# First cross-attention of a two-layer kernel: scores and values on parts of the TensorE array, spreading on GpSimd, half of the normalising on ScalarE, another order of the steps

## The reference

```python
def _layernorm(x, axis=-1, eps=1e-05):
    m = jnp.mean(x, axis=axis, keepdims=True)
    v = jnp.var(x, axis=axis, keepdims=True)
    return (x - m) / jnp.sqrt(v + eps)

def _L0_xattn_ref(x, y, Wq, bq, Wkv, bkv, Wo, bo):    # x: 2x1024x256, y: 2x77x192, 16 heads of 16
    q = (jnp.einsum('bld,ed->ble', x, Wq) + bq).reshape(b, l, h, dh)
    kv = (jnp.einsum('bmc,ec->bme', y, Wkv) + bkv).reshape(b, m, h, 2 * dh)
    k, v = (kv[..., :dh], kv[..., dh:])
    att = jax.nn.softmax(jnp.einsum('blhd,bmhd->blmh', q, k) * scale, axis=2)
    out = jnp.einsum('blmh,bmhd->blhd', att, v).reshape(b, l, d)
    return jnp.einsum('bld,ed->ble', out, Wo) + bo
# x = x + attention(layernorm(x)), then x = x + experts(layernorm(x)), and the second layer
```

## Time and profile before

| | before |
|---|---|
| runs, median (lowest to highest) | 885.86 us (884.95 to 891.11), 3 runs |
| profiled execution, its own time | 889.84 us |
| its span | 887.7 us |
| busy in the span | PE 724.3 us, DVE 584.6, POOL 355.8, ACT 294.8 |

### The profile page before, as it was taken

The page is one execution under the profiler, slowest core; times in us unless marked ns, Lnnn a source line. Parts: engine busy times, 40 slices in busy tenths (PEclk is TensorE's granted clock), DMA queues, the critical chain, the costliest instruction groups (busy, mean ns, idle before and its releaser), DMA issues.

```text
span 887.7 us, 10616 instructions
## 1 busy us (share of the span) xinstructions
PE 724.3 (82%) x3332; PEld 417.2 (47%) x3332; DVE 584.6 (66%) x1732; ACT 294.8 (33%) x641; POOL 355.8 (40%) x372
## 2 busy tenths in 40 slices
PE   4689877864798998989979866868798899999972
PEld 3456544562344444444547623323253374647651
DVE  3888887435756373462657788999795497664265
ACT  2354333210372451815412253555420212021210
POOL 2344434103588685685410246787700021112020
PEclk9999999955898997988979977998889799999996
DMA  8910000210122221121288100020010000000002
GB/s 219 400 31 1 1 12 3 80 62 24 53 72 72 69 81 49 65 81 58 78 256 317 44 2 0 1 95 1 0 48 0 1 1 0 1 0 1 0 1 95
DMA packets 33086, 52.77 MB, mean 59 GB/s; under 512 B 8718, under 2 KB 21582, under 8 KB 32776
## 3 DMA queue, kind: packets, MB, share of 16 engines
q1 hardware_dynamic: 28040, 36.76, 12.6%
q0 software_dynamic: 4992, 15.34, 5.1%
HBM read 36.62 MB, written 15.47 MB: 59 GB/s over the span
## 4 chain that ended last, share of the span: by engine, by line
PE 54%; DVE 25%; POOL 6%; issue 6%; ACT 5%; DMA 2%; POOLq 1%; SPq 0%; DVEq 0%; ACTq 0%
PE ps L459 50%; DVE arena L1883 4%; DVE arena L1880 3%; ACT arena L934 2%; DVE arena L1496 2%; DVE arena L1492 2%; DVE arena L329 2%; DMA arena<-scr_z,idsU 2%; DVE kp L1385 1%; DVE arena L1385 1%; DVE arena L1391 1%; POOL arena L1274 1%; POOL scr_g L1266 1%; PE ps L514 1%; DVE X L1391 1%
## 5 line engine op out<-in xcount | busy, mean ns | idle before, releaser
L459 PE MATMUL ps<-arena 64*32 64x32 f32 (+6 forms) x2296 | 543.6, 396 | 29.9 <-DVE arena L1609 8.7
L459 PEld LDWEIGHTS ps<-arena 128*128 128x128 f32 (+3 forms) x2296 | 267.3, 164 | 231.5 <-issue 182.7
L934 ACT ACTIVATE arena<-ps 128x256 f32<-128x256 f32 (+6 forms) x255 | 120.5, 487 | 280.5 <-PE ps L459 136.0
L324 POOL TENSOR_SCALAR rstd<-mv 128x4 f32<-128x4 f32 (+2 forms) x34 | 14.6, 430 | 236.8 <-DVE mv L318 183.4
L1736 DVE TENSOR_TENSOR arena<-ps,arena 128x512 f32<-128x512 f32 x39 | 27.0, 691 | 103.3 <-ACT arena L1048 91.1
L1232 POOL TENSOR_TENSOR arena<-arena 128x616 f32<-128x616 f32 x32 | 40.2, 1256 | 80.0 <-DVE arena L1504 80.0
L1266 POOL DMA_INDIRECT scr_g<-arena,destU x39 | 50.1, 1285 | 37.7 <-DVE arena L1736 30.4
L1259 POOL DMA_INDIRECT arena<-scr_z,idsU x39 | 45.9, 1177 | 40.8 <-PE ps L652 28.7
L1883 DVE MATCH_REPLACE8 arena<-arena 128x77 f32<-128x77 f32 x256 | 54.1, 222 | 0.0
L1048 ACT ACTIVATE arena<-ps 128x512 f32<-128x512 f32 x39 | 23.3, 597 | 92.2 <-PE ps L459 92.0
L988 ACT ACTIVATE arena<-arena 128x616 f32<-128x616 f32 x32 | 23.0, 717 | 75.7 <-DVE arena L1496 75.7
(11 more groups left out here) (196 smaller groups left out, 988.9 us busy)
## 6 DMA issues: line engine op xcount, KB each, us to landing
arena<-in_w1t SPq DMA_DIRECT2D x8, 1024.0 KB, 14.0
arena<-scr_g SPq DMA_DIRECT2D x8, 1024.0 KB, 7.9
X<-in_x SPq DMA_DIRECT2D x2, 1024.0 KB, 5.9
scr_z<-arena SPq DMA_DIRECT2D x4, 512.0 KB, 3.3
...
```

The lines of the kernel that those rows point to most:

```text
L459: return pe.matmul(o, l, r, start=first, stop=final)
L934: return a.activation(o, i, ACT.Copy)
```

## The change

Scores: each of the two matmuls of a unit takes only the 64 rows of `qT` and `kblk` that aren't zero for its four heads, so one lies on partitions 0 to 63 and the other on 64 to 127. Values: instead of five matmuls with 128 output columns, eight with 32 output columns (two heads) each, over the two chunks that hold those heads' keys; their outputs lie on the four groups of 32 PSUM partitions. All values of a group are now in one place of the order. The first spreads of the keys (batch 0) stay on DVE; the other six go to GpSimd, ahead of its loop, with a semaphore of their own (`vblk_ready`). `kvT` shares the memory of `OT`. `norm_A` of blocks 2 and 3 and `norm_B` of blocks 0 and 1 move to ScalarE as activations with scale rstd and bias -mean x rstd (`nmr`), which GpSimd prepares in `ln_shift`. ScalarE has `put_P` ahead of the exponential; DVE has sum and reciprocal of u - 1 (`total`) ahead of the maximum of u. `queries(0, 1)` and several of the other parts stand at other steps, and `project`'s second pair goes to bank 6 of its own. In the diff below `turn_P`'s buffer index (PBUF, still 4) is left out, and so are removed lines that the functions above show.

```diff
@@ -48,6 +48,8 @@
...
+LAG = 3
+PBUF, LATE = LAG + 1, LAG - 2
...
@@ -144,10 +146,10 @@
...
-        Pb = ra.take(4, GW)
-        kvT = Region(ra.at).take(2, 2, NB * S2)
+        Pb = ra.take(PBUF, GW)
...
-        mxA, smA = ra.take(4, HG), ra.take(4, HG)
+        mxA, smA, nmr = ra.take(PBUF, HG), ra.take(PBUF, HG), ra.take(2 * TB)
+        kvT = OT.rearrange("p g n -> p (g n)")[:, 0:4 * NB * S2].rearrange("p (a b n) -> p a b n", a=2, b=2)
...
@@ -496,10 +498,11 @@
                     pe.wait_ge(s["scores_read"], u - 1)
                 if t == 0:
                     pe.wait_ge(s["qT_sb"], 2 * j + g + 1)
-                    pe.wait_ge(s["kblk_ready"], 2 if j < 2 else 8)
+                    pe.wait_ge(*((s["kblk_ready"], 2) if j < 2 else (s["vblk_ready"], 6)))
                 for c in range(2):
-                    ins = mm(ps[:, 2 * (u % 2) + c, 0:BW], qT[:, j % 2, g, t * P:(t + 1) * P],
-                             kblk[:, g, j // 2, c * BW:(c + 1) * BW], True, True)
+                    half = slice(c * P // 2, (c + 1) * P // 2)
+                    ins = mm(ps[:, 2 * (u % 2) + c, 0:BW], qT[half, j % 2, g, t * P:(t + 1) * P],
+                             kblk[half, g, j // 2, c * BW:(c + 1) * BW], True, True)
                 ins.then_inc(s["scores_ready"], 1)
             def turn_P(u):
@@ -525,26 +528,21 @@
                     ins = pe.transpose(ps[0:m, 6, c * P:(c + 1) * P], vblk[:, g, b, ch * P:ch * P + m], ident[:])
                 ins.then_inc(s["vk_ps"], 1)
...
+            def values(j, g):
+
+                pe.wait_ge(s["pt_sb"], turned_all(8 * j + 4 * g + 3))
+                for r in range(2):
+                    for q in range(4):
+                        m, cols = vkeys(q + r), slice(32 * q, 32 * q + 32)
+                        ins = mm(ps[cols, 6, :], vk[0:m, j // 2, g, q + r, cols], PT[0:m, g, q + r, :], r == 0, r == 1)
+                ins.then_inc(s["oT_ps"], 1)
             def project(j, pair):
                 pe.wait_ge(s["oT_sb"], 2 * j + 2)
...
                 for t in (2 * pair, 2 * pair + 1):
                     for g in range(2):
...
+                        ins = mm(ps[:, 6 + pair, (t % 2) * D:(t % 2) * D + D], OT[:, g, t * P:(t + 1) * P], wo0[:, g, :],
                                  g == 0, g == 1)
                 ins.then_inc(s["oA_ps"], 1)
@@ -553,55 +551,61 @@
             turn_z(0, 0, 7)
             turn_z(0, 1, 6)
             queries(0, 0, 7)
...
+            for S in range(NU + LAG):
                 j, st = S // 8, S % 8
                 ahead = j + 1 < NBLK
                 if S < NU:
                     scores_A(S)
...
+                if S >= LAG:
+                    turn_P(S - LAG)
                 if 1 <= S <= 5:
                     turn_v(S - 1)
...
+                if S >= NU:
+                    pass
+                elif st == 0:
                     if j >= 2:
...
+                        pe.wait_ge(s["xA_done"], 2 * j - 2)
+                    else:
+                        pe.wait_ge(s["qT_sb"], 1 + 2 * j)
+                    queries(j, 1, 7)
+                elif st == 1 and ahead:
+                    pe.wait_ge(s["qT_sb"], 2 * j + 2)
+                    turn_z(j + 1, 0, 7)
+                    if j:
+                        pe.wait_ge(s["oT_sb"], 2 * j - 1)
+                        turn_z(j + 1, 1, 6)
                 elif st == 2:
...
+                    if j == 0:
+                        pe.wait_ge(s["zTA_sb"], 3)
+                        turn_z(1, 1, 7)
+                    elif ahead:
+                        queries(j + 1, 0, 7)
+                elif S == 3:
+                    queries(1, 0, 7)
+                j, st = (S - LATE) // 8, (S - LATE) % 8
+                ahead = j + 1 < NBLK
+                if j < 0 or S >= NU + LATE:
+                    continue
+                if st == 2 and j:
                     if ahead:
...
+                        pe.wait_ge(s["zTA_sb"], 2 * j + 4)
+                    else:
+                        pe.wait_ge(s["oT_sb"], 2 * j - 1)
+                    values(j - 1, 1)
+                elif st == 4 and j:
+                    project(j - 1, 0)
+                elif st == 5 and j:
                     if ahead:
...
+                        pe.wait_ge(s["qT_sb"], 2 * j + 3)
+                    project(j - 1, 1)
                 elif st == 6:
                     if j:
...
+                        pe.wait_ge(s["xA_done"], 2 * j - 1)
+                    else:
+                        pe.wait_ge(s["vk_sb"], 5)
+                    values(j, 0)
+            pe.wait_ge(s["oT_sb"], 2 * NBLK - 1)
+            values(NBLK - 1, 1)
             project(NBLK - 1, 0)
             project(NBLK - 1, 1)
             stage_end("tensor", pe)
@@ -976,34 +980,57 @@
                     a.wait_ge(s["oA_ps"], 2 * j)
                 copy(OT[:, g, :], bank(6)).then_inc(s["oT_sb"], 1)
+            def scaled(dst, n, k):
+                return a.activation(dst, X[:, n, :], ACT.Identity, bias=nmr[:, k:k + 1], scale=rstd[:, k:k + 1])
+
+            def norm_A2(j, tiles):
+                a.wait_ge(s["lnA_rstd"], j + 1)
+                a.wait_ge(s["zTA_ps"], 2 * j)
+                for t in tiles:
+                    scaled(zA[:, t, :], 4 * j + t, 4 * (j % 2) + t).then_inc(s["zA_ready"], 1)
+
+            def norm_B2(j, tiles):
+                a.wait_ge(s["lnB_rstd"], j + 1)
+                for t in tiles:
+                    scaled(zB[:, 4 * j + t, :], 4 * j + t, TB + 4 * j + t).then_inc(s["zB_ready"], 1)
+
             for i in range(2):
                 put_z(0, i, 7 - i)
...
+            put_q(0, 0, 7)
+            for S in range(NU + LAG):
                 j, st = S // 8, S % 8
                 ahead = j + 1 < NBLK
+                if S >= LAG:
+                    put_P(S - LAG)
+                if 1 <= S <= 5:
+                    put_v(S - 1)
                 if S < NU:
                     a.wait_ge(s["scores_read"], S + 1)
...
+                    a.activation(Pb[:, S % PBUF, :], Pb[:, S % PBUF, :], ACT.Exp, scale=1.0 / math.sqrt(DH0))\
                         .then_inc(s["probs_exp"], 1)
...
+                    if st == 0:
+                        put_q(j, 1, 7)
+                    if st == 1 and ahead:
+                        put_z(j + 1, 0, 7)
+                        if j:
+                            put_z(j + 1, 1, 6)
+                    if st == 2 and ahead:
+                        if j:
+                            put_q(j + 1, 0, 7)
+                        else:
+                            put_z(1, 1, 7)
                     if S == 3:
...
+                        put_q(1, 0, 7)
+                    if (S - LATE) % 8 == 2 and j:
                         put_o(j - 1, 1)
...
+                    if (S - LATE) % 8 == 6:
+                        put_o(j, 0)
+                    if S in (6, 7):
+                        norm_A2(2, (2 * (S - 6), 2 * (S - 6) + 1))
+                    elif S in (11, 12):
+                        norm_A2(3, (2 * (S - 11), 2 * (S - 11) + 1))
+                    elif j >= 2 and st in (3, 4) and "B" in stages:
+                        norm_B2(j - 2, (2 * (st - 3), 2 * (st - 3) + 1))
             put_o(NBLK - 1, 1)
             stage_end("scalar", a)
             if "B" in stages:
@@ -1212,11 +1239,27 @@
             own.done(p.memset(halfpi[:], math.pi / 2))
             own.settle()
+            def ln_shift(at, stats, count, signal):
+                r, m = rstd[:, at:at + 4], nmr[:, at:at + 4]
+                p.wait_ge(s[stats], count)
+                own.done(p.tensor_scalar(r, mv[:, at:at + 4, 1], EPS, None, ALU.add))
+                own.done(p.tensor_scalar(m, mv[:, at:at + 4, 0], -1.0, None, ALU.mult))
+                own.settle()
+                own.done(p.tensor_tensor(r, r, neghalf[:, 0:4], ALU.pow))
+                own.settle()
+                p.tensor_tensor(m, m, r, ALU.mult).then_inc(s[signal], 1)
+
             def rstd_A(j):
-                ln_rstd(p, own, 4, 4 * (j % 2), "lnA_stats", j + 1, "lnA_rstd")
+                if j < 2:
+                    ln_rstd(p, own, 4, 4 * (j % 2), "lnA_stats", j + 1, "lnA_rstd")
+                else:
+                    ln_shift(4 * (j % 2), "lnA_stats", j + 1, "lnA_rstd")
             def rstd_B(j):
-                ln_rstd(p, own, 4, TB + 4 * j, "lnB_stats", j + 1, "lnB_rstd")
+                if j >= 2:
+                    ln_rstd(p, own, 4, TB + 4 * j, "lnB_stats", j + 1, "lnB_rstd")
+                else:
+                    ln_shift(TB + 4 * j, "lnB_stats", j + 1, "lnB_rstd")
             def bias_A(T):
@@ -1225,20 +1268,32 @@
             rstd_A(0)
             rstd_A(1)
+            p.wait_ge(s["consts_in"], 16 * 9)
+            p.wait_ge(s["kv_sb"], 4)
+            for i, b in ((1, 0), (1, 1), (0, 1)):
+                for g in range(2):
+                    p.tensor_tensor((kblk, vblk)[i][:, g, b, :].rearrange("p (h k) -> p h k", h=HG),
```

(64 more changed lines are left out.)

119 lines of the change are left out of this document (3 added, 116 removed).

## The result

| | before | changed |
|---|---|---|
| runs, median (lowest to highest) | 885.40 us (882.58 to 891.11), 4 runs | 862.48 us (861.03 to 864.02), 4 runs |
| profiled execution, its own time | 889.84 us | 861.57 us |
| its span | 887.7 us | 859.6 us |
| first maximum of the loop | 25.91 | 23.29 |
| end of the last subtraction | 150.98 | 132.45 |

The ratio is 0.973, with a 95% interval of 0.968 to 0.979: faster by 22.9 us, where 18.6 were forecast. The last three rows of the table split what happened in stage A of the two profiled executions: run-up 25.91 - 23.29 = 2.6 us less, loop 125.1 to 109.2, 15.9 less, tail 20.2 to 17.7, 2.5 less; together 21.1 us. Behind stage A the profiled executions differ by another 7.0 us (716.5 and 709.5). Before's profiled execution lies 4.0 us above the median of its first runs, so a part of the 7.0 may be that; what makes them up was not isolated.

What follows compares the result with a forecast made beforehand. It took PE to bound the loop, with DVE close behind and the new bound after the change. 23.1 us saved less 4.5 for the clock gave 18.6 us saved, 867.3 us, with a range of 858 to 880.

Steps and rivals of the forecast that it cites:

- the sum: Whole kernel: 23.1 us saved in the stage, less 4.5 for the clock, so 18.6 us saved and 867.3 us.
- the likeliest case: Whole kernel: the forecast as summed, 864 to 872 us, chance 0.6.
- DVE's cycle: Loop: sum, reciprocal, maximum, subtraction and exponential repeat every 3.35 us, with a 0.79 us hole on DVE.
- PE's work after the change: Loop: with tiles fully overlapping, scores 0.51 us and values 1.72, a block takes 19.9 us, 2.5 a step.
- the mechanism that the prediction made of it: PE: tiles in program order barely overlap, scores 0.77 us, values 3.9, 3.3 a step; within a rival of chance 0.18.
- such a cost at a change of the tiling mode: PE: two or three drains of 0.27 us a step would lift 2.5 us to at most 3.3.
- Extras: DVE in the loop: `split_bias` 6.0 us and statistics 1.3 beyond the holes, 7.3 in all.
- The clock in the loop: Loop: PE's granted clock may fall in steps 25, 26 and 28, costing 0 to 6 us, 1.5 taken.
- Run-up: Before the loop: scores wait only for the first query copy, so the first maximum comes at 23.1 us instead of 25.91.
- ScalarE's queue: Loop: copies and normalisations (0.4 us each) ahead of or behind the exponential delay nothing, at most 1 us.
- Tail: From the last subtraction to the next stage's first transposes: 12.2 us against 20.2, before any clock cost.
- the clock's cost: Tail: values and projections at half the clock, bounds 0 and 5.5 us, 3 taken.

Runs made afterwards that it cites:

- e12: The changed kernel again, with only a blank line ahead of it: 858.85 us, ratio 0.971 to the kernel before.
- e11: The kernel before with six spreads moved to GpSimd, norms to ScalarE, and tiled scores and values, in the old orders: 867.39 us, ratio 0.977.
- e4: The changed kernel with four idle 512-column matmuls added on PE in the tail: 854.58 us, ratio 0.966 to the kernel before.
- e6: The changed kernel with the sixteen normalisations moved from ScalarE back to DVE: 864.92 us, ratio 0.973 to the kernel before.
- e7: The changed kernel with the six spreads moved from GpSimd back to DVE: 863.31 us, ratio 0.973 to the kernel before.
- e3: The kernel before with only the tiled scores and values added: 886.01 us, ratio 0.999 to the kernel before.
- e9: The kernel before with only six spreads moved to GpSimd and the norms to ScalarE, no tiles, old orders: 876.22 us, ratio 0.988.
- e8: The changed kernel with ScalarE's exponential back ahead of the copies (`put_P`): 873.04 us, ratio 0.985 to the kernel before.
- e2: The changed kernel with DVE's sum and reciprocal of u-1 back behind the subtraction of u: 851.42 us, ratio 0.962 to the kernel before.

## Why the prediction was right, step by step

The time lies in the range of 858 to 880, 4.8 us below the 867.3 of the sum and 1.5 below the likeliest case of 864 to 872. How it comes about was forecast in the main: a loop set by DVE's cycle of sum, maximum, subtraction and exponential. But the number didn't test the tiles: without them (e1) it would have been 867.0, in the likeliest case itself. By its steps:

- **PE's work after the change.** Four tiles side by side: forecast 1.72 us for the values and 1.9 with the end, measured 1.93; two row tiles: 0.51 of work and 0.82 with the end, measured 0.79. That the tiles overlap is shown. The Trainium skill, "TensorE: Matmul & The Clock Gate", Part 3, has matmuls start and end strictly in program order; the mechanism that the prediction made of it, 3.9 and 0.77 plus the end, is not what these tiles do. But PE's work was put too low, at 1.06 us for scores and transposes of a step, where 0.72 + 0.69 = 1.41 pass from start to start. That is 0.35 a step and 2.8 a block, so 22.7 us a block where 19.9 were forecast. It shows in the busy time: 85% of the loop, part of it at the lower clock, where 70 to 80 were forecast, and 29.64 of 35.00 us at a granted clock of 0.98. The prediction allowed for such a cost at a change of the tiling mode as an upper bound and left it out of the sum. How much of the 0.35 comes from that change no run isolates. In the changed kernel it showed no cost: DVE waited for PE 0.6 us in all.
- **DVE's cycle.** Forecast 3.35 with a hole of 0.79, measured 3.31 with 0.78, and waits for PE down to 0.6 us: right. The 15.6 us of waits that the prediction read from the earlier trace rows were only 8.9 in the loop; the first, 6.7, belongs to the run-up.
- **Extras.** 7.3 us forecast beyond the cycles, 109.16 - 31 x 3.31 - 1.63 = 4.9 measured. `split_bias` was sized from rows that had stood beside GpSimd's work: 7.7, where it took 5.6 here. The clock in the loop, 1.5 taken, showed no cost on DVE; at 0.92 PE was still ahead. The loop so came out 5.1 us shorter than the sum: 1.2 of it from the cycle, 2.4 from the extras, 1.5 from the clock.
- **Run-up.** 23.1 forecast, 23.29 measured (22.36 in e12). GpSimd's six spreads took the 7.3 us that were forecast. But DVE's normalisations beside them took 4.98 us for four, where they took 1.38 before, which the prediction didn't price. It delayed nothing here, since DVE still waited 0.63 us for the scores; in e11 the same four ended at 23.93 us and the first maximum came right behind them, so a little of it was luck.
- **ScalarE's queue.** The normalisations cost 0.54 each, not 0.4, within their bounds, and nobody waited for them.
- **Tail.** 12.2 without the clock's cost; e4 shows 12.6 at full clock. With it 17.7 in the profiled execution: the clock cost 5 us there, near the upper bound of 5.5, where 3 was taken. In e12 it cost 2.2, in e6 and e7 2.8 and 2.3. So 3 was a fair middle, and the first profile's 5 is one execution; in it the tail made up for a part of the loop.
- **What the sum didn't say.** 18.6 us against 21.1 in stage A. The start, "bound by PE, with DVE close behind", leaned too far to PE: e3 relieves PE alone and gains nothing clear (1.1 us), e9 relieves DVE alone and gains 10.5, and the two together give 20.5 (e11). e8 shows that, with the change's order on DVE, copies first is worth 9.5 us of the loop. The move of the sum ahead of the maximum, which the prediction only priced at the new cycle, is a loss of 7.8 us in the loop and of 8 to 11 in the time (e2 against e12 and against the changed kernel).
- **The rest of the program.** "As long as before" was forecast; 7.0 us less were seen in the profiled executions, and the cause stays open. The gain at stage A's end and that of the medians (21.1 and 22.9) agree within the 4 us by which two executions of the changed kernel differ there.
